# A decoder layer's self attention: the order of the softmax work, of the residual addition and of one unit's transposes

## The chip, the cores and the metric

One core of one Trainium2 chip runs the whole kernel. The metric is the device time of one execution in microseconds; the kernel before is timed three times and its median is taken.

## The reference, cut to what matters

A pre-norm decoder layer on a batch of 32 sequences of 64 tokens, width 512, in float32. It has three parts, each added to the residual x: causal self attention (32 query heads of 16, 8 key heads), cross attention over a context of 64 tokens (32 query heads of 128, 8 key heads, RMS norm of queries and keys), and a feed-forward part with routing. The change is in the first:

```
x = x + attn(layernorm(x), wq, wk, wv, wo)
x = x + cross(layernorm(x), ctx, mask, ...)
x = x + ffn(layernorm(x), ...)

# attn:
scores = einsum('bihd,bjhd->bhij', q, k) * SCALE     # 16 per head, k repeated 4 times
scores = where(causal, scores, finfo.min)
attn   = softmax(scores, axis=-1)
out    = einsum('bhij,bjhd->bihd', attn, v).reshape(b, s, 512) @ wo
```

## The kernel before

The batch is worked in two halves of 16 sequences (1024 tokens, 8 tiles of 128). Each half goes through projections and context transposes, self attention, cross attention (a loop over 8 key heads) and the feed-forward part. Products keep float32 precision by splitting each operand into a high and a low part, so one product is three matmuls (`split_mm`, lines 429 to 431).

Every engine has a list of instructions in program order, written out by hand; an engine waits at a semaphore with all that stands behind it in its list. Self attention is a loop over `p`, one step for each sequence of the half (`NSEQ` = 16), and each engine has its own version of this loop in `self_attention(half)`. A sequence has two units, `2p` and `2p + 1`: the first 32 queries, which see 32 keys (128x256 elements in all), and the last 32, which see all 64 keys (128x512). I call them even and odd units. A unit goes this way:

- TensorE: `scores1(b)`, both units of a sequence, two steps ahead (`AHEAD` = 2), L653 and L657.
- ScalarE: `copy_scores`, L1124, out of the accumulation banks into one of six buffers of `prob`.
- VectorE: `unit_max`, L1562. GpSimd: `unit_subtract_max`, L1930. ScalarE: `unit_exps`, L983. VectorE: `unit_sums`, L1567 and a reciprocal, L1570. GpSimd: `unit_normalise`, L1936.
- TensorE: `transpose_probs`, L470, into one bank (`pt1`) that both units use in turn. ScalarE: `evacuate_probs`, L987. TensorE: `values1`, L675.

After two sequences the output of a token tile is complete: ScalarE's `output_hi` (L990) and VectorE's `output_lo` (L1354) split it, and TensorE projects it in four parts (`project_part`, called from `behind(p, 0)` and `behind(p, 1)`, `y<-w_hi`), two in each of two steps from step 4 on. All these projections use one bank, `y[0]`. VectorE's `updated` (L1574) adds the bank to x and frees it (`y_free`); the first part of the next tile waits for that. From step 7 on VectorE also computes the second layer norm's statistics (`second_statistics`, L1362 to L1367, odd steps) and applies it (`second_norm`, L1584, even steps), with a reciprocal root on GpSimd (L1909) and transposes on TensorE (L689, odd steps from 9). GpSimd's list also splits two weight pieces of the next stage in eight strips (`split_strip`, L1903, steps 5 to 12), and ScalarE casts four pieces (L970, after steps 0, 2, 4 and 7).

In the second half, the projections before self attention are in `second_projections`. There VectorE's list has the low parts of the context tiles (`contexts_lo`, L1354) and two first layer norms (`first_norm(1, 6)` and `first_norm(1, 7)`, L1374). TensorE's transposes of context tiles 4 and 5 (L447) wait for the low parts of tiles 2 and 3, since they use the same two banks.

Of the kernel before, what the change touches and what calls it, by code (L numbers as in the profile page):

```python
# [22 lines left out]
NSEQ = HALF // SEQ  # L23
# [16 lines left out]
AHEAD = 2  # L40
# [80 lines left out]
def decoder_block(nc, x_in, ctx_in, mask_in, w_self, w_cross, qn_in, kn_in, w_ffn,  # L121
                  f1g_in, expt_in, fc2_in, gamma_in, beta_in, out):
    with ExitStack() as stack:
# [164 lines left out]
        def evacuated(eng, at, n):  # L288

            eng.wait_ge(acc_free[n % 2].sem, at(acc_free[n % 2], n // 2 + 1))  # L290
# [136 lines left out]
        def _(pe):  # L427
# [192 lines left out]
            def self_attention(half):  # L620
# [93 lines left out]
                pe.wait_ge(gaps_clear.sem, at(gaps_clear, 1))  # L714

                for p in range(NSEQ + 1):
                    if p + AHEAD < NSEQ:
                        scores1(p + AHEAD)
                    if p >= 1:
                        values1(2 * p - 2)  # L720
                        values1(2 * p - 1)
                    if p == 0:
                        behind(0, 0)
                        evacuated(pe, at, A1[half]["kt1"])
                    if p < NSEQ:
                        transpose_probs(at, 2 * p, (2 * p) % URING)
                    if p > 0:
                        behind(p, 0)
                    else:
                        behind(0, 1)  # L730
                    if p < NSEQ:
                        transpose_probs(at, 2 * p + 1, (2 * p + 1) % URING)
                    if p > 0:
                        behind(p, 1)
                    if p >= 9 and p % 2 == 1:
                        second_norm((p - 9) // 2)
# [228 lines left out]
        def _(act):  # L965
# [19 lines left out]
            def evacuate_probs(at, u, buffer):  # L985
                act.wait_ge(pt_rdy.sem, at(pt_rdy, u + 1))
                nc.scalar.copy(probt[:, buffer, :], pt1).then_inc(pt_done.sem, 1)  # L987
# [116 lines left out]
            def self_attention(half):  # L1104
                place = Place(1, half)
                at = place.at
                def spread_values(b):

                    if b == 0:
                        act.wait_ge(zone_clear.sem, 1)  # L1110
                        act.wait_ge(proj_out.sem, at(proj_out, PROJ[half]["kv3"] + 1))
                    if b >= 4:
                        act.wait_ge(pv_done.sem, at(pv_done, 2 * b - 6))
                    rows = slice((b % 2) * SEQ, (b % 2 + 1) * SEQ)
                    values = kv[rows, b // 2, P:2 * P].rearrange("p (i g d) -> p g i d", i=4, g=2)
                    for g2 in range(2):
                        ins = nc.scalar.copy(own_block(b % 4, g2), values[:, g2])
                    ins.then_inc(vbd_done.sem, 1)

                def copy_scores(u):  # L1120

                    act.wait_ge(sc_rdy.sem, at(sc_rdy, u // 2 * 2 + 2))
                    target = seen(u, u % URING).rearrange("p (i g) k -> p i g k", i=4)
                    nc.scalar.copy(target, far if u % 2 else near).then_inc(s_add.sem, 1)  # L1124

                spread_values(0)
                spread_values(1)
                if half == 0:
                    act.wait_ge(wqk_made.sem, 1)

                    act.wait_ge(f1g_lo_done.sem, 1)
                self_queries(half, 4)
                def second_norm_hi(i):
                    act.wait_ge(solo_rdy.sem, at(solo_rdy, SOLO[f"lx{i}"] + 1))
                    nc.scalar.copy(tile_of(xn_hi, i), blocks(solo)).then_inc(ln_hi_done.sem, 1)

                for p in range(-AHEAD, NSEQ + 1):
                    scored = p + AHEAD < NSEQ
                    if p == -1:
                        self_queries(half, 5)  # L1140
                    if scored:
                        copy_scores(2 * (p + AHEAD))
                        copy_scores(2 * (p + AHEAD) + 1)
                    if 0 <= p < NSEQ:
                        evacuate_probs(at, 2 * p, 0)
                    if scored:
                        unit_exps(at, 2 * (p + AHEAD))
                    if p >= 2 and p % 2 == 0:
                        i = (p - 2) // 2
                        act.wait_ge(pv_done.sem, at(pv_done, 4 * i + 4))  # L1150
                        output_hi(i)
                    if 0 <= p < NSEQ:
                        evacuate_probs(at, 2 * p + 1, 1)
                    if scored:
                        unit_exps(at, 2 * (p + AHEAD) + 1)
                    if p in (1, 3):
                        self_queries(half, 6 + p // 2)
                    if p >= 9 and p % 2 == 1:
                        second_norm_hi((p - 9) // 2)
                    if 0 <= p < NSEQ - 2:  # L1160
                        spread_values(p + 2)
                    if p in (0, 2, 4, 7):

                        n = (0, 2, 4, 7).index(p)
                        if n > 1:
                            act.wait_ge(solo_rdy.sem, at(solo_rdy, 2))
                        else:
                            act.wait_ge(proj_rdy.sem, at(proj_rdy, 8))
                        split_piece(Place(2, half, 0), n)

                first = Place(2, half, 0)
                second_norm_hi(4)
                keys_and_values(first, 0)
                second_norm_hi(5)
                queries(first, 0, 0)
                queries(first, 0, 1)
                second_norm_hi(6)
                keys_and_values(first, 1)
                queries(first, 1, 0)
                sibling_keys(first.at, 0)  # L1180
                queries(first, 1, 1)
                exps(first.at, 0, 0)
                keys_and_values(first, 2)
                sibling_keys(first.at, 1)
                queries(first, 2, 0)
                queries(first, 2, 1)
                second_norm_hi(7)
# [163 lines left out]
        def _(dve):  # L1351
# [107 lines left out]
            def first_norm(half, i):  # L1459
                normalise(Place(1, half).at, 0, i, A1[half][f"ln{i - 2}"] if i >= 2 else None)  # L1460
# [44 lines left out]
            def second_projections():  # L1505
                norms_lo(1, 4)
                contexts_lo(1, 0)
                first_statistics(1, 6)
                first_statistics(1, 7)
                first_norm(1, 6)  # L1510
                first_norm(1, 7)
                contexts_lo(1, 2)
                contexts_lo(1, 4)
                norms_lo(1, 6)
                contexts_lo(1, 6)
# [30 lines left out]
            def self_attention(half):  # L1546
# [44 lines left out]
                first = Place(2, half, 0)  # L1591
                for p in range(-AHEAD, NSEQ + 1):
                    scored = p + AHEAD < NSEQ
                    if scored:
                        unit_max(2 * (p + AHEAD))
                        unit_max(2 * (p + AHEAD) + 1)
                    if p >= 6 and p % 2 == 0:
                        updated((p - 6) // 2)
                    if p >= 11 and p % 2 == 1:
                        second_norm_lo((p - 11) // 2)  # L1600
                    if scored:
                        unit_sums(2 * (p + AHEAD))
                    if p >= 2 and p % 2 == 0:
                        output_lo(at, (p - 2) // 2)
                    if scored:
                        unit_sums(2 * (p + AHEAD) + 1)
                    if p >= 7 and p % 2 == 1:
                        second_statistics((p - 7) // 2)
                    if p >= 8 and p % 2 == 0:
                        second_norm((p - 8) // 2)  # L1610
                    if p in (1, 3):
                        weights_lo(first, p // 2)
# [271 lines left out]
        def _(pool):  # L1884
# [104 lines left out]
            def self_attention(half):  # L1989
# [15 lines left out]
                for p in range(-AHEAD, NSEQ):  # L2005
                    scored = p + AHEAD < NSEQ
                    if scored:
                        unit_subtract_max(at, 2 * (p + AHEAD))
                        unit_subtract_max(at, 2 * (p + AHEAD) + 1)
                    if p >= 8 and p % 2 == 0:  # L2010
                        layernorm_rstd(at, NT, (p - 8) // 2)
                    if scored:
                        unit_normalise(at, 2 * (p + AHEAD))
                        unit_normalise(at, 2 * (p + AHEAD) + 1)
                    if 5 <= p < 13:
                        split_strip(Place(2, half, 0), 2 + (p - 5) // 4, (p - 5) % 4)

# [158 lines left out]
```

## Time and profile before

| | us |
|---|---|
| median of 3 runs | 1632.32 (1631.72 to 1632.89) |
| the profiled execution | 1631.22 |
| its span | 1629.5 |
| TensorE busy in the span | 1572.7 (97%) |
| VectorE, ScalarE, GpSimd busy | 1107.5, 749.3, 618.9 |

The self attention loops lie at 57 to 141 us and 861 to 946 us of the span. Busy time of TensorE is that of pipelined matmuls, whose ends are modelled, so that it hides short pauses. A line in brackets behind a timeline row is the idle time of the engine before that instruction, and what ended it.

### The profile page before, as it was taken

What the parts mean: (1) busy time and instruction counts of PE and PEld (TensorE: products, weight loads), DVE (VectorE), ACT (ScalarE), POOL (GpSimd) and SP (SyncE); (2) the same over time, 40 slices, a digit from 0 to 9 for tenths busy, and PEclk for the clock granted to TensorE, in tenths of its full rate; (3) what the DMA queues carried; (4) which work ended last, traced back from release to release, by engine and by line L of the source; (5) the groups of instructions that cost most, each with busy time, mean ns of one, the idle gap of its engine ahead of it and who ended that gap; (6) DMA issues with size and microseconds to landing.
All of it is one profiled execution on the core that took longest, in us unless ns stands there. A gap on an engine that the chain in (4) does not pass through costs nothing.

```text
span 1629.5 us, 42096 instructions
## 1 busy us (share of the span) xinstructions
PE 1572.7 (97%) x17432; PEld 1317.1 (81%) x17432; DVE 1107.5 (68%) x1965; ACT 749.3 (46%) x1398; POOL 618.9 (38%) x523
## 2 busy tenths in 40 slices
PE   7879999999999999999997799999999999999998
PEld 6557888888888888789885588888888888887897
DVE  6666857667676676785666667667666766768844
ACT  4674535535444444431237645444444544544321
POOL 5573424324243342551227724333243242424501
PEclk9999999999999999999999899999999999999999
DMA  6100202012020120131120002011020110202100
GB/s 226 39 15 7 67 2 65 19 45 64 0 64 19 45 64 6 40 111 52 66 78 27 18 5 67 14 51 57 7 64 6 58 45 19 71 0 66 41 19 27
DMA packets 26289, 71.63 MB, mean 44 GB/s; under 512 B 3168, under 2 KB 3424, under 8 KB 26208
## 3 DMA queue, kind: packets, MB, share of 16 engines
q1 hardware_dynamic: 26208, 70.48, 13.6%
q8 instruction: 60, 0.98, 0.2%
q14 instruction: 21, 0.17, 0.0%
HBM read 66.27 MB, written 4.19 MB: 43 GB/s over the span
## 4 chain that ended last, share of the span: by engine, by line
PE 87%; DVE 4%; POOL 4%; ACT 3%; issue 1%; DMA 0%; SPq 0%; POOLq 0%; ACTq 0%; DVEq 0%
PE acc L429 14%; PE acc L430 13%; PE acc L431 13%; PE y L429 10%; PE y L431 10%; PE y L430 10%; PE quad L781 6%; PE quad L810 4%; PE y L794 2%; POOL prob L1930 2%; POOL prob L1936 1%; ACT prob L983 1%; DVE psum_ L1567 1%; PE acc L447 1%; PE quad L429 1%
## 5 line engine op out<-in xcount | busy, mean ns | idle before, releaser
L429 PE MATMUL y<-w_hi 128*128 128x512 f32 x576 | 231.8, 402 | 23.2 <-DVE x L1574 22.5
L1909 POOL TENSOR_TENSOR qkrs<-qkve,mhalf 128x10 f32<-128x10 f32 x64 | 125.0, 1953 | 302.3 <-DVE qkve L1531 302.3
L431 PE MATMUL y<-w_hi,w_lo 128*128 128x512 f32 x576 | 226.1, 392 | 0.0
L430 PE MATMUL y<-w_lo,w_hi 128*128 128x512 f32 x576 | 225.9, 392 | 0.0
L429 PE MATMUL acc<-w_hi,xn_hi 128*128 128x512 f32 x512 | 207.1, 405 | 0.0
L430 PE MATMUL acc<-w_lo,xn_hi 128*128 128x512 f32 x512 | 201.2, 393 | 0.0
L431 PE MATMUL acc<-w_hi,xn_lo 128*128 128x512 f32 x512 | 199.5, 390 | 0.0
L1430 DVE TENSOR_TENSOR x<-y,x 128x512 f32<-128x512 f32 x128 | 88.3, 690 | 140.3 <-PE y L431 140.3
L1890 POOL TENSOR_TENSOR w_lo<-stage,w_hi 128x1024 fp32r<-128x1024 f32 (+1 forms) x80 | 156.5, 1965 | 62.8 <-ACT w_hi L970 58.8
L1525 DVE TENSOR_REDUCE qkss<-kk 128x4 f32<-128x512 f32 x128 | 87.3, 682 | 103.9 <-ACT kk L1009 103.3
L970 ACT CAST w_hi<-stage 128x1024 fp32r<-128x1024 f32 (+1 forms) x116 | 105.1, 918 | 98.0 <-PE y L431 63.8
L429 PE MATMUL acc<-w_hi,cx_hi 128*128 128x256 f32 x512 | 149.8, 293 | 0.0
L429 PEld LDWEIGHTS y<-w_hi 128*128 128x128 f32 x576 | 109.0, 189 | 48.0 <-issue 23.2
L1918 POOL TENSOR_TENSOR prob<-prob,pmax 128x512 f32<-128x512 f32 x64 | 69.3, 1083 | 201.0 <-DVE pmax L1413 201.0
L431 PE MATMUL acc<-w_hi,cx_lo 128*128 128x256 f32 x512 | 144.9, 283 | 0.0
L430 PE MATMUL acc<-w_lo,cx_hi 128*128 128x256 f32 x512 | 144.8, 283 | 0.0
L1202 ACT COPY probt<-y 128x512 f32<-128x512 f32 x64 | 37.6, 587 | 215.9 <-PE y L794 215.9
L431 PEld LDWEIGHTS y<-w_hi,w_lo 128*128 128x128 f32 x576 | 109.0, 189 | 23.1
L429 PEld LDWEIGHTS acc<-w_hi,xn_hi 128*128 128x128 f32 x512 | 96.0, 187 | 38.7 <-issue 19.2
L430 PEld LDWEIGHTS y<-w_lo,w_hi 128*128 128x128 f32 x576 | 109.2, 190 | 19.9
L1924 POOL TENSOR_TENSOR prob<-prob,prec 128x512 f32<-128x512 f32 x64 | 66.8, 1044 | 153.2 <-DVE prec L1421 153.2
L1008 ACT COPY qb<-acc 128x512 f32<-128x512 f32 x128 | 75.3, 588 | 101.7 <-PE acc L431 98.9
(167 smaller groups left out, 3853.8 us busy)
## 6 DMA issues: line engine op xcount, KB each, us to landing
stage<-in_w_cross SPq DMA_DIRECT2D x64, 512.0 KB, 3.7
stage<-in_w_cross SPq DMA_DIRECT2D x32, 256.0 KB, 2.8
stage<-in_w_ffn SPq DMA_DIRECT2D x16, 512.0 KB, 3.5
stage<-in_w_self SPq DMA_DIRECT2D x8, 512.0 KB, 5.6
out_x<-x SPq DMA_DIRECT2D x16, 256.0 KB, 2.0
x<-in_x SPq DMA_DIRECT2D x6, 512.0 KB, 5.4
kk<-in_ctx SPq DMA_DIRECT2D x8, 256.0 KB, 4.2
prob<-in_ctx SPq DMA_DIRECT2D x8, 256.0 KB, 4.2
```

The source lines that it names most:

```text
L429: nc.tensor.matmul(target, l_hi, r_hi, start=first, stop=False)
L430: nc.tensor.matmul(target, l_hi, r_lo, start=False, stop=False)
L431: return nc.tensor.matmul(target, l_lo, r_hi, start=False, stop=last)
L781: ins = nc.tensor.matmul(quad[h * SEQ:(h + 1) * SEQ, i, t * SEQ:(t + 1) * SEQ], q2t[rows, t, j, 2 * h:2 * h + 2, :].rearrange("p h q -> p ...
L970: nc.scalar.copy(target, stage[:, place.slot(n), 0:width]).then_inc(w_hi_done, 1)
L1008: nc.scalar.copy(qraw[:, 2 * (k % 2) + t], blocks(acc[n % 2]))
L1430: nc.vector.tensor_tensor(x[:, i % NT, :], y[i % 2][:], x[:, i % NT, :], ALU.add).then_inc(y_free.sem, 1)
L1525: nc.vector.tensor_reduce(qkss[:, k % 2, t * REP:(t + 1) * REP], qsq[:, t], AX_X, ALU.add).then_inc(q_sum.sem, 1)
L1890: nc.gpsimd.tensor_tensor(low, stage[:, place.slot(n), 0:width], high.bitcast(F32), ALU.subtract).then_inc(w_lo_done, 1)
L1909: return nc.gpsimd.tensor_tensor(target, source, mhalf[:, 0:width], ALU.pow)
L1918: nc.gpsimd.tensor_tensor(pr, pr, spread(pmax[:, buffer, :], 8, SEQ), ALU.subtract).then_inc(s_sub.sem, 1)
L1924: nc.gpsimd.tensor_tensor(pr, pr, spread(prec[:, buffer, :], 8, SEQ), ALU.mult).then_inc(s_nrm.sem, 1)
```

## The change

Nothing is computed in another way, and no instruction is added or removed. What moves:

- VectorE: `updated` and `second_norm_lo` stand first in the step, ahead of both maxima. The sums of the odd unit are taken one step later.
- TensorE: `scores1(p + 2)` stands behind the even unit's transposes, not at the head of the step. In step 0 two parts of a query projection stand first.
- ScalarE: the even unit's `evacuate_probs` stands ahead of `copy_scores`; the odd unit's exponential moves to the next step, ahead of the even unit's.
- GpSimd: the odd unit's `unit_normalise` moves to the next step, between the two subtractions.
- Second half's projections: `contexts_lo(1, 2)` stands ahead of the two `first_norm`.

```
 TensorE    for p in range(NSEQ + 1):
-                    if p + AHEAD < NSEQ:
-                        scores1(p + AHEAD)
+                    if p == 0:
+                        behind(0, 0)
+                        evacuated(pe, at, A1[half]["kt1"])
+
                     if p >= 1:
                         values1(2 * p - 2)
                         values1(2 * p - 1)
-                    if p == 0:
-                        behind(0, 0)
-                        evacuated(pe, at, A1[half]["kt1"])
                     if p < NSEQ:
                         transpose_probs(at, 2 * p, (2 * p) % URING)
-                    if p > 0:
+                    if p + AHEAD < NSEQ:
+                        scores1(p + AHEAD)
+                    if p == 0:
+                        behind(0, 1)
+                    else:
                         behind(p, 0)
-                    else:
-                        behind(0, 1)
                     if p < NSEQ:
                         transpose_probs(at, 2 * p + 1, (2 * p + 1) % URING)
 ScalarE
+                    if 0 <= p < NSEQ:
+                        evacuate_probs(at, 2 * p, 0)
                     if scored:
                         copy_scores(2 * (p + AHEAD))
                         copy_scores(2 * (p + AHEAD) + 1)
-                    if 0 <= p < NSEQ:
-                        evacuate_probs(at, 2 * p, 0)
-                    if scored:
-                        unit_exps(at, 2 * (p + AHEAD))
+                    if 0 <= p + 1 < NSEQ:
+                        unit_exps(at, 2 * (p + 1) + 1)
...
                     if scored:
-                        unit_exps(at, 2 * (p + AHEAD) + 1)
+                        unit_exps(at, 2 * (p + AHEAD))
 VectorE, second_projections
+                contexts_lo(1, 2)
                 first_norm(1, 6)
                 first_norm(1, 7)
-                contexts_lo(1, 2)
 VectorE, self_attention
-                    if scored:
-                        unit_max(2 * (p + AHEAD))
-                        unit_max(2 * (p + AHEAD) + 1)
+
                     if p >= 6 and p % 2 == 0:
                         updated((p - 6) // 2)
                     if p >= 11 and p % 2 == 1:
                         second_norm_lo((p - 11) // 2)
                     if scored:
-                        unit_sums(2 * (p + AHEAD))
+                        unit_max(2 * (p + AHEAD))
+                    if 0 <= p + 1 < NSEQ:
+                        unit_sums(2 * (p + 1) + 1)
+                    if scored:
+                        unit_max(2 * (p + AHEAD) + 1)
                     if p >= 2 and p % 2 == 0:
                         output_lo(at, (p - 2) // 2)
                     if scored:
-                        unit_sums(2 * (p + AHEAD) + 1)
+                        unit_sums(2 * (p + AHEAD))
 GpSimd
                         unit_subtract_max(at, 2 * (p + AHEAD))
-                        unit_subtract_max(at, 2 * (p + AHEAD) + 1)
                     if p >= 8 and p % 2 == 0:
                         layernorm_rstd(at, NT, (p - 8) // 2)
+                    if 0 <= p + 1 < NSEQ:
+                        unit_normalise(at, 2 * (p + 1) + 1)
                     if scored:
+                        unit_subtract_max(at, 2 * (p + AHEAD) + 1)
                         unit_normalise(at, 2 * (p + AHEAD))
-                        unit_normalise(at, 2 * (p + AHEAD) + 1)
```

## Rows read from the trace of the kernel before

**Rows 1.** Stretch behind the loop: length, busy us PE PEld DVE ACT POOL (instructions), clock
```profile
143.00:164.00 21.00, 21.00 (x123) 18.43 (x123) 12.86 (x29) 9.25 (x19) 3.06 (x3) 1.00 0.00 1
```
**Rows 2.** The same view: both loops, and a slice of the first
```profile
56.60:141.00 84.40, 66.23 (x817) 46.95 (x810) 53.79 (x130) 59.42 (x135) 57.84 (x73) 0.96 0.08 23
860.70:946.50 85.80, 68.02 (x818) 48.33 (x810) 53.78 (x130) 59.58 (x136) 57.87 (x74) 0.92 0.08 23
...
100.00:110.00 10.00, 9.35 (x109) 6.84 (x110) 5.53 (x14) 6.27 (x15) 6.32 (x9) 0.83 0.18 52
```
**Rows 3.** TensorE's waits, first half's loop: total us, times, longest
```profile
PE y L429 <- DVE x L1574: 11.4, 5, 3.4
```
**Rows 4.** Chain that ended last, steps 0 and 1: start, us, what
```profile
60.91 1.58 POOL prob L1930 x2
62.52 0.64 ACT prob L983
63.18 0.70 DVE psum_ L1567
64.18 1.04 POOL prob L1936
```
**Rows 5.** The same chain, steps 9 to 11
```profile
104.86 1.23 POOL prob L1936
...
116.18 1.23 POOL prob L1936
```
**Rows 6.** ScalarE's timeline: start, us, instruction, [idle before, releaser]
```profile
51.14 0.86 ACT L1124 COPY prob<-quad 128x256 f32<-128x256 f32 x2 [0.53 <-PE quad L657]
...
61.84 0.57 ACT L987 COPY probt<-acc 128x512 f32<-128x512 f32 x1
...
95.45 0.57 ACT L987 COPY probt<-acc 128x512 f32<-128x512 f32 x1
...
139.30 0.59 ACT L987 COPY probt<-acc 128x512 f32<-128x512 f32 x1 [0.81 <-PE acc L470]
```
**Rows 7.** TensorE's timeline, first half
```profile
50.26 0.45 PE L653 MATMUL quad<-kk,qb 32*128 32x64 f32 x8
...
62.46 0.43 PE L675 MATMUL acc<-probt,vbd 128*32 128x128 f32 x8 [0.53 <-ACT probt L987]
...
89.24 0.47 PE L429 MATMUL y<-w_hi 128*128 128x512 f32 x1 [1.52 <-DVE x L1574]
...
90.01 0.60 PE L470 MATMUL acc<-ident,prob 128*128 128x128 f32 x4
90.36 0.48 PE L429 MATMUL y<-w_hi 128*128 128x512 f32 x1
...
91.98 0.64 PE L675 MATMUL acc<-probt,vbd 128*32 128x128 f32 x16
92.55 0.66 PE L470 MATMUL acc<-ident,prob 128*128 128x128 f32 x4
```
**Rows 8.** VectorE's timeline, first half
```profile
88.41 0.68 DVE L1574 TENSOR_TENSOR x<-y,x 128x512 f32<-128x512 f32 x1
...
97.64 0.64 DVE L1362 BATCH_NORM_STATS2 bn<-x 128x6 f32<-128x512 f32 x1
...
98.66 1.17 DVE L1562 TENSOR_REDUCE pmax<-prob 128x8 f32<-128x256 f32 x2
```
**Rows 9.** Timelines of TensorE, VectorE, GpSimd, second half's projections
```profile
839.46 1.22 PE L447 MATMUL acc<-ident,kk 128*128 128x128 f32 x8 [1.41 <-DVE cx_lo L1354]
...
835.12 0.55 DVE L1374 TENSOR_SCALAR xn<-x,mv,rstd 128x512 f32<-128x512 f32 x1
836.10 2.60 DVE L1374 TENSOR_SCALAR xn<-x,mv,rstd 128x512 f32<-128x512 f32 x1 [0.44 <-POOL rstd L1909]
...
836.04 2.38 POOL L1890 TENSOR_TENSOR w_lo<-stage,w_hi 128x1024 fp32r<-128x1024 f32 x1
```
**Rows 10.** GpSimd's timeline, first half
```profile
68.49 1.39 POOL L1936 TENSOR_TENSOR prob<-prob,prec 128x512 f32<-128x512 f32 x1 [0.86 <-DVE prec L1570]
```

## The prediction, made before the changed kernel ran

> **What bounds the kernel now.** I read the page first: TensorE is busy for 1572.7 of 1629.5 us, so time can come only from its pauses and from stretches at a low clock. The busy time by stretch shows where these lie: in the two self attention loops TensorE is busy for 66.23 of 84.40 us and for 68.02 of 85.80 us, so it is idle for 18.2 and 17.8 us [rows 2]. In the first loop the list of waits gives the largest part, 11.4 us in five waits of up to 3.4 us, to VectorE's addition to the residual, which frees the one bank of the projections [rows 3]. Such a pause also costs clock: in the slice that holds a pause of 3.4 us the granted clock is 0.83, a part of it at 1.2 instead of 2.4 GHz, and over the whole loops it is 0.96 and 0.92 [rows 2].
>
> The chain of waits shows why VectorE is late. In the first steps it never touches TensorE: GpSimd subtracts the maxima of two units (1.58), ScalarE takes the odd unit's exponential (0.64), VectorE sums it (0.70 and 0.30 to GpSimd's start), GpSimd normalises it (1.04), and only then comes the next subtraction: 1.6 + 0.7 + 1.0 + 1.0 = 4.3 us for one step, in series [rows 4]. Late in the loop two steps take 116.18 - 104.86 = 11.3 us [rows 5], 5.7 each. TensorE is not needed for a step longer than about 4 us: values 0.57, transposes 0.35 to 0.4 twice, scores 0.8 (a little less than the 0.88 from their start to their copy at 51.14, [rows 6]), two parts of a projection at 0.77 each [rows 7] make 3.7.
>
> I take as the clock of the loop ScalarE's copy of the odd unit's transposes (the odd copy). Before, it starts at 61.84 in step 0, at 95.45 in step 7 and at 139.30 in step 15 [rows 6]: 33.6 us for seven steps and 43.9 for eight.
>
> **The odd unit's end one step later.** GpSimd's list is now: subtract even, normalise the last odd, subtract odd, normalise even. The odd unit's exponential and sum run beside two GpSimd instructions of the next step. What is left in series for an odd unit is subtraction 1.0, exponential 0.66, sum 1.0, normalisation 1.0, 3.7 us [rows 4], 0.6 less than before, and it starts a step earlier than it is needed. GpSimd's own work, 57.8 us in 16 steps [rows 2], is 3.6 a step and no longer sets the pace, but leaves little slack.
>
> Next late are ScalarE and TensorE in turn. After an odd copy: 0.62 to the values (61.84 to 62.46, [rows 6, 7]), 0.57 for them, 0.4 for the even transposes, 0.88 from the scores' start to their copy (50.26 to 51.14, [rows 6, 7]), then on ScalarE two score copies and the odd exponential (0.86 and 0.64, of which about 0.2 overlap: 1.3), then the next odd copy. That is 3.8 us; in an even step the output's high part, a copy like the odd copy (0.6, less 0.1 of overlap), stands in between: 4.3. Seven steps: 3 x 4.3 + 4 x 3.8 = 28.1; with ScalarE's weight casts behind steps 0, 2 and 4, mostly beside TensorE's values, I take 28.3. Gain 5.3 us.
>
> **Step 0.** Two query parts stand first and fill the pause in which the scores wait for a copy. The first odd copy now waits for GpSimd: normalise unit 1, subtract unit 3, then ScalarE's exponential. I put it at 60.0 instead of 61.84. Gain 1.9. The even unit 2 is normalised later than before and still ahead of its transposes; with that cover gone each microsecond there would count once.
>
> **The addition first.** The change takes two maxima (1.17, [rows 8]), and what they wait for, from in front of it. Still in front of it stands the end of VectorE's odd step: the even unit's sum and the statistics (97.64 to 98.66, 1.0, [rows 8]). So the wait for it does not vanish from step 8 on. From the odd copy: 0.75 until the even exponential starts (behind the odd copy on ScalarE), 0.45 for it and 0.6 for the sum with its reciprocal (estimates, from 0.64 and 0.70 for the odd unit's twice as many elements, [rows 4]), 0.2 behind the odd maximum, 1.0 for the statistics, 0.83 from the addition's start to TensorE (88.41 to 89.24, [rows 7, 8]), 0.77 for the part, 0.66 for the transposes until the next odd copy [rows 7]: 5.3 us for an even step. TensorE alone would need some 1.2 us less, so I expect four waits of 1.1 to 1.7 us, none in step 6, which has no statistics in front. An odd step is TensorE's own, 3.7 and 0.1 of hops, 3.8; the last, without scores, 3.0. Steps 8 to 15: 5.5 (a weight cast in front) + 5.4 + 5.3 + 4.8 (no scores) + 3 x 3.8 + 3.0 = 35.4. Gain 43.9 - 35.4 = 8.5. The pauses get too short for the low clock: the 1.52 us one in front of 89.24 left the next matmul at 0.47 [rows 7].
>
> The even transposes in front of the scores cost nothing as long as their unit is normalised, and it is, two steps ahead. The scores start some 0.4 us later after them; this is in the 0.4 above. No DMA is issued by any step that moves. The weight strips on GpSimd and the second norm's transposes are in the steps as before; behind the loop TensorE is busy for all of 21 us [rows 1], so nothing waits there that VectorE could bring earlier.
>
> **One half, the other half.** 1.9 + 5.3 + 8.5 = 15.7 us for the first loop. The second is 1.4 us longer, at the lower clock [rows 2]; without the low clock it loses that too: 17.1. In the second half's projections TensorE waits 1.41 us for the low parts of the context [rows 9]; with these in front of the two norms the wait goes, 1.4. The norms move back by some 0.6 us beside the same long GpSimd instruction (836.04, 2.38 us), which sets the second's end rather than the order [rows 9]. Sum 34.2.
>
> From this I take 4 for what the rows show once and the sum has not: GpSimd's normalisation takes 1.39 us instead of 1.04 beside some VectorE instructions [rows 4, 10], which I put at 0.25 in eight steps of each loop. An estimate, bounded by 0 and by 0.35 x 32 steps = 11.
>
> The bounds of the whole: all idle time of both loops, 36.0, the 1.4, and up to 5 of clock (the loops' lower clock took 1.8 more busy time in the second than in the first [rows 2]) would be 42.4; below, the early gain alone, 2 x 7.2 less 1 of clock, 13. Forecast 34.2 - 4 = 30. The profiled execution took 1631.22, so 1601.2; its median stands 1.1 above, so **1602.3 us**.
>
> **Rivals.** *TensorE fills up*: hops overlap better and the waits for the addition go wholly. For it: no engine but TensorE needs over 4 us a step. Against: statistics stand in front of the addition. Gain 41, 1591 us.
>
> *The addition stays late*: the wait of even steps keeps its length because the even unit's sum, which now waits for an exponential behind two copies, comes as late as both maxima did. For it: the serial 5.3 us is an addition of hops, each of which may be short. Then the late gain is gone: 13 to 14, 1618 us.
>
> *No change that can be told*: the loop is paced by something that isn't moved. Only ScalarE's work, 59.4 us in 84.4 [rows 2], comes near, and it leaves 25. 1632.
>
> *Slower: VectorE and GpSimd get into each other's way.* Before, GpSimd stands idle when VectorE writes the second norm (L1584); after, it is busy some 85% of the loop (57.8 of about 69). A write of the same size and kind took 0.55 us beside an idle GpSimd, and 2.60 when a GpSimd instruction of 2.38 us had begun 0.06 before it [rows 9]. If each of the 16 in the two loops is drawn out by 2.05, on the path, that is 33 us and eats the whole gain: 1632.3 - 30 + 33 = 1635. It decides at a mean of about 2.4 us for L1584. Against: GpSimd's instructions in the loop last 1.04 at most, and these writes stand in even steps' ends, in front of a maximum with slack.
>
> The Trainium skill, GPSIMD Engine Reference, section "Key points", says that GpSimd shares its SBUF interfaces with VectorE and is in contention with VectorE instructions that run in a 2-port mode or have two SBUF inputs. The trace agrees in the 2.60 against 0.55; by that rule as a full lock the slower rival would hold, and by the rows' length of GpSimd's instructions in the loop, 1.04 at most, it costs half of that or less.
>
> **Chances.** Forecast 0.62, fills up 0.15, addition stays late 0.13, no change 0.03, slower 0.07. Range 1590 to 1620: it takes in the fuller and the late rival and leaves out no change and slower, and a tenth in sum. What this kernel's measurement can tell from no change is about 0.2%, 3.3 us. Faster by more: 0.90; within: 0.03; slower by more: 0.07.
>
> **What would show it.** Odd copies of the first half at about 60, 88 and 124 us, against 61.84, 95.45 and 139.30; the loop's end near 125. Waits of TensorE for L1574: four of 1.1 to 1.7 in each half, about 5.5 in all. Granted clock 1.00 in both loops. No wait of L447 for the low context parts in the second half. GpSimd without its 0.86 us wait in front of each odd normalisation [rows 10]. Wrong: if even steps take 6 us or more, if L1584 is over 1.5 us in the mean, or if time is given back behind the loop, where TensorE has no pause now [rows 1].

## The result and the profile after

The changed kernel takes 1616.59 us in the median of five runs (1615.12 to 1625.62), against 1632.32: ratio 0.992, 95% interval 0.9906 to 0.9934. By the interval it is faster by 11 to 15 us, by the medians by 15.7; forecast were 30, to 1602.3. The median lies in the range of 1590 to 1620, but about half of the forecast gain is missing. A second set of six runs of the same kernel had a median of 1621.64 (1613.32 to 1628.65).

The profiled execution is the slowest of the first five, 1625.62 us. TensorE's waits in both loops, from the list of waits of the kernel after (what waits and for what: us in total, times, longest); the lines of the page and of the code are one to three higher than before, so L1575 is the addition, L1355 the subtraction behind `output_lo`, L675 the values:

```profile
PE acc L675 <- DVE w_lo L1355: 16.9, 12, 2.2
PE y L429 <- DVE x L1575: 8.6, 8, 1.6
PE acc L675 <- ACT probt L988: 2.9, 4, 1.1
```

The waits for the addition have shrunk from 22.5 us in both loops (11.4 in the first, [rows 3]) to 8.6, a little below the forecast of some 5.5 in each. A wait that was 1.0 us in all before is now the largest: TensorE's values (the products of probabilities and values, `values1`) wait for VectorE's low part of the output, 16.9 us in twelve waits. In step 3 of the first half it looks like this, in ScalarE's timeline:

```profile
66.99 0.63 ACT L984 ACTIVATE prob<-prob 128x512 f32<-128x512 f32 x1 [0.26 <-POOL prob L1933]
67.53 0.57 ACT L991 CAST w_hi<-acc 128x512 fp32r<-128x512 f32 x1
```

in VectorE's:

```profile
67.65 0.69 DVE L1568 TENSOR_REDUCE psum_<-prob 128x8 f32<-128x512 f32 x1 [0.96 <-ACT prob L984]
...
68.49 0.63 DVE L1563 TENSOR_REDUCE pmax<-prob 128x8 f32<-128x512 f32 x1
69.04 0.68 DVE L1355 TENSOR_TENSOR w_lo<-acc,w_hi 128x512 fp32r<-128x512 f32 x1
```

and in TensorE's:

```profile
69.87 0.96 PE L675 MATMUL acc<-probt,vbd 128*32 128x128 f32 x16 [2.15 <-DVE w_lo L1355]
70.76 1.12 PE L470 MATMUL acc<-ident,prob 128*128 128x128 f32 x4
```

The values of a new tile go into the bank that holds the output of the last one, and may not start until both of its parts are out. The high part now stands behind the odd unit's exponential on ScalarE; the low part stands behind that unit's sum and the next odd maximum on VectorE, so that it starts 0.94 us after the high part's end (68.10 to 69.04). In the kernel before, at the same place, ScalarE, VectorE and TensorE had:

```profile
70.81 0.57 ACT L990 CAST w_hi<-acc 128x512 fp32r<-128x512 f32 x1
```

```profile
71.51 0.64 DVE L1354 TENSOR_TENSOR w_lo<-acc,w_hi 128x512 fp32r<-128x512 f32 x1
```

```profile
72.30 0.65 PE L675 MATMUL acc<-probt,vbd 128*32 128x128 f32 x16 [0.24 <-DVE w_lo L1354]
```

There the low part also had two maxima and a sum in front of it, but both maxima were done at 70.07 and the sum was the even unit's, so the low part started 0.13 us behind the high one. Behind the pause of 2.15 us the values take 0.96 and the transposes 1.12 us instead of 0.64 and 0.66 [rows 7]. The busy time by stretch shows a low granted clock there (bounds, length, busy us of PE, PEld, DVE, ACT, POOL, granted clock, DMA):

```profile
70.00:80.00 10.00, 10.00 (x106) 7.21 (x101) 4.16 (x10) 5.63 (x13) 5.16 (x7) 0.66 0.06 12
80.00:90.00 10.00, 8.20 (x76) 5.52 (x75) 5.61 (x13) 6.46 (x15) 5.90 (x8) 0.69 0.11 44
```

The odd copies of steps 0, 7 and 15, which were the clock of the prediction [rows 6], in ScalarE's timeline:

```profile
59.57 0.57 ACT L988 COPY probt<-acc 128x512 f32<-128x512 f32 x1
...
98.78 0.59 ACT L988 COPY probt<-acc 128x512 f32<-128x512 f32 x1
...
137.54 0.59 ACT L988 COPY probt<-acc 128x512 f32<-128x512 f32 x1 [0.81 <-PE acc L470]
```

59.6, 98.8 and 137.5 where 60, 88 and 124 were expected. Steps 0 to 2 are within half a microsecond of the working (63.32 and 67.99 follow); from step 3 on the measured steps are longer.

### The profile page after: what moved, and what is told of

Same layout as the page of the kernel before. It is cut to its first block, busy times and chain, and to the rows that moved or that the text cites. A ratio compares the mean times of both kernels' runs of the same rounds, so it can differ in the third digit from the quotient of the medians.

```text
span 1623.9 us, 42096 instructions
## 1 busy us (share of the span) xinstructions
PE 1578.9 (97%) x17432; PEld 1322.4 (81%) x17432; DVE 1106.5 (68%) x1965; ACT 748.8 (46%) x1398; POOL 619.0 (38%) x523
## 4 chain that ended last, share of the span: by engine, by line
PE 92%; DVE 3%; ACT 3%; issue 1%; POOL 1%; DMA 0%; SPq 0%; POOLq 0%; ACTq 0%; DVEq 0%
PE acc L429 14%; PE acc L430 13%; PE acc L431 13%; PE y L429 10%; PE y L430 10%; PE y L431 10%; PE quad L782 6%; PE quad L811 4%; PE y L795 2%; PE acc L470 1%; PE quad L653 1%; PE acc L447 1%; PE quad L429 1%; PE acc L675 1%; PE quad L431 1%; PE quad L430 1%
```

## Experiments

All times are medians, set against runs of the kernel before on the same chip: 1631.89 us for the first four, 1631.23 for the last four.

**The changed kernel once more.** No edit.

> The changed kernel as it is. Its five times lay from 1615.1 to 1625.6 us, and the profiled execution was the slowest, with granted clock 0.66 to 0.69 in two slices of the first loop. Theory A: the spread is the low clock, which some executions catch behind the 2 us waits for output_lo in steps 3 and 5; then another execution of about 1615 us shows the same waits of TensorE (L1355 some 16 us in both loops, L1575 some 9) and a granted clock near 1.00 in the loops, which are then some 4 to 5 us shorter each. Theory B: the waits themselves differ between executions, and the clock is only a mark of it.

Measured: 1621.64 us (1613.32 to 1628.65, six runs), ratio 0.9942 (0.9919 to 0.9965). Time and the mean granted clock of the execution go together: 1613.32 and 1614.76 at 0.999, 1621.25 and 1622.02 at 0.993, 1626.6 at 0.990, 1628.65 at 0.988. The profiled execution was the fastest. Its waits, and its two loops by busy time:

```profile
PE acc L675 <- DVE w_lo L1355: 15.8, 12, 2.1
PE y L429 <- DVE x L1575: 10.0, 10, 1.6
```

```profile
54.00:142.00 88.00, 73.58 (x881) 54.29 (x882) 60.51 (x150) 62.88 (x143) 59.90 (x76) 0.98 0.08 23
857.00:947.00 90.00, 76.68 (x880) 58.47 (x877) 61.18 (x148) 60.87 (x138) 57.36 (x72) 1.00 0.07 22
```

The same stretches in the profile of 1625.62 us:

```profile
54.00:142.00 88.00, 73.66 (x865) 53.08 (x858) 57.39 (x138) 61.51 (x140) 59.22 (x75) 0.92 0.07 22
857.00:947.00 90.00, 75.86 (x861) 55.42 (x861) 58.74 (x144) 60.04 (x137) 58.86 (x74) 0.91 0.07 22
```

The same twelve waits of up to 2.2 us in both profiled executions, with a loop clock of 0.98 and 1.00 in one and of 0.92 and 0.91 in the other. Theory A holds for these two: the waits are there both times, the clock falls behind those of steps 3 and 5 in one and not in the other. The times of one and the same kernel spread over 15 us. The fastest execution is 18.6 us below the median of the kernel before (whose mean clock is 0.991 to 0.994), the slowest 3.2.

**The output's split earlier.**

```
 ScalarE
+   output_hi(i)                                # with its wait
     if 0 <= p + 1 < NSEQ: unit_exps(at, 2 * (p + 1) + 1)
-   output_hi(i)
 VectorE
     if scored: unit_max(2 * (p + AHEAD))
+   output_lo(at, (p - 2) // 2)
     if 0 <= p + 1 < NSEQ: unit_sums(2 * (p + 1) + 1)
     if scored: unit_max(2 * (p + AHEAD) + 1)
-   output_lo(at, (p - 2) // 2)
```

> The changed kernel with the output's split earlier: ScalarE's output_hi ahead of the odd unit's exponential, VectorE's output_lo ahead of the odd unit's sum and maximum. Theory A (the missing gain lies in TensorE's wait for output_lo, 16.9 us in twelve waits, and in the low clock that the long ones bring): that wait falls below 3 us, odd steps take 3.8 to 4.0 us instead of 4.9, and the time is 1600 to 1606 us. Theory B (the odd steps are bound by the softmax chain itself, and the wait for output_lo only stands in front): the wait moves to the odd unit's copy or its transposes, and the time stays at 1612 to 1616.

Measured: 1600.87 us (1599.00 to 1601.06), ratio 0.9804 (0.9791 to 0.9816), clock 0.997 to 0.999 in every run. The list of waits, then TensorE's timeline at the values of step 3, then ScalarE's odd copies:

```profile
PE y L429 <- DVE x L1575: 10.8, 10, 1.6
PE acc L675 <- ACT probt L988: 2.9, 4, 1.1
PE acc L675 <- DVE w_lo L1355: 1.2, 4, 0.3
```

```profile
67.55 0.74 PE L675 MATMUL acc<-probt,vbd 128*32 128x128 f32 x16 [0.33 <-DVE w_lo L1355]
```

```profile
59.03 0.57 ACT L988 COPY probt<-acc 128x512 f32<-128x512 f32 x1
...
87.72 0.59 ACT L988 COPY probt<-acc 128x512 f32<-128x512 f32 x1
...
125.61 0.59 ACT L988 COPY probt<-acc 128x512 f32<-128x512 f32 x1 [0.81 <-PE acc L470]
```

The wait falls from some 16 us to 1.2, and the time to that of the forecast: 31 us gained. Theory A holds. Against the two executions of the changed kernel at a mean clock of 0.999 (1613.32 and 1614.76) it is 12 to 14 us, near the 14.6 us of waiting that are gone (15.8 to 1.2); what the medians show beyond that goes with the clock. The odd copies at 59.0, 87.7 and 125.6 lie close to the 60, 88 and 124 of the prediction. Step 11 takes 3.9 us from odd copy to odd copy (103.90 to 107.84), where the changed kernel has 4.9 (113.92 to 118.82). What ScalarE's part of this edit brings alone was not measured.

The low clock has become rarer and is not gone. TensorE's timeline and the stretch around it:

```profile
91.77 0.47 PE L429 MATMUL y<-w_hi 128*128 128x512 f32 x1 [1.48 <-DVE x L1575]
```

```profile
90.00:100.00 10.00, 8.52 (x94) 6.16 (x92) 6.58 (x18) 7.53 (x17) 7.79 (x11) 0.83 0.08 17
```

**Only the low part, ahead of the odd maximum.** In VectorE's list `output_lo` changes places with `unit_max(2 * (p + AHEAD) + 1)`; ScalarE as in the change.

> The changed kernel with VectorE's output_lo ahead of the odd unit's maximum only (0.55 us earlier); ScalarE unchanged. Theory A: each of the twelve waits for output_lo shrinks by 0.55, 6.6 us in all, more where that also keeps the clock up: 1606 to 1610 us. Theory B (the maximum, now 0.6 us later, holds up GpSimd's subtraction and so the step): no gain, 1615 or more.

Measured: 1605.87 us (1605.41 to 1607.81), ratio 0.9841 (0.9828 to 0.9854), clock 0.998 to 1.000. That is 8 us below the changed kernel at its high clock, close to the 6.6 of twelve half microseconds, and 11 to 16 below its medians, which have the low clock in them. Waits:

```profile
PE y L429 <- DVE x L1575: 10.0, 10, 1.6
PE acc L675 <- ACT vbd L1118: 5.9, 4, 1.6
PE acc L675 <- DVE w_lo L1355: 3.0, 6, 0.9
```

The values wait for 5.9 + 3.0 us here, 6.9 less than the 15.8 at high clock. The profile puts four of these waits to copies of values into `vbd`, which belong to a later sequence. In step 3 the low part ends at 68.57 and the values start at 68.72, the same 0.15 us after it as in the changed kernel (69.72 and 69.87), so I read them as waits for it. One maximum, 0.63 us long, has moved by one place: theory A, and a dose between nothing and the experiment before.

**The addition first, alone.** The kernel before, with `updated` and `second_norm_lo` ahead of both maxima.

> The kernel before with one part of the change alone: VectorE's addition to the residual (and second_norm_lo) ahead of both maxima. Theory A: it takes the two maxima, 1.0 us, and what they wait for from ten waits of 22.5 us, and leaves the sum and the statistics in front; the softmax ring of 5 us a step stays: 8 to 12 us gained, 1620 to 1624 us, some from the clock. Theory B (the ring of the softmax sets late steps too, the wait for the addition moves to the odd unit's transposes): under 4 us, 1628 to 1632.

Measured: 1626.37 us (1624.84 to 1627.43), ratio 0.9964 (0.9952 to 0.9977). Waits:

```profile
PE y L429 <- DVE x L1574: 16.4, 10, 2.3
PE acc L470 <- ACT probt L987: 5.0, 7, 1.0
```

Between the theories: 5.5 us gained, from 6.1 us less of waiting for the addition. The waits shrink by 0.6 us each rather than by the 1.0 of the two maxima; the even unit's sum and the statistics stand in front as before. The waits for the low part grow from 1.0 to 2.5 us.

**The second half's context edit, alone.** The kernel before, with `contexts_lo(1, 2)` ahead of the two norms.

> The kernel before with the edit of the second half's projections alone (low parts of context tiles 2 and 3 ahead of two layer norms). Theory A: TensorE's wait of 1.4 us there goes and nothing else moves: 1630.0 to 1631.0 us against 1631.9, at the edge of what can be told; in the profile L447 waits for L1354 no more. Theory B: the time is given back at the next transposes, 1631.9.

Measured: 1632.03 us (1627.60 to 1634.10, eleven runs), ratio 0.9998 (0.9988 to 1.0007). The wait of 1.41 us [rows 9] is in no list of waits of this kernel or of the changed one, but the time can't be told from before; the interval allows a gain of up to 2.0 us, so 1.4 is neither shown nor excluded in the whole time. The granted clock of its runs is 0.989 to 0.993, and their times spread over 6.5 us. In the profiles the gain can be seen: from the transposes in front of the ones that waited to the first even copy of the second half's loop it is 29.35 us before (834.26 to 863.61) and 27.54 here (837.06 to 864.60), so up to the loop nothing of it is given back.

**The statistics behind the addition.** The kernel with the output's split early, and VectorE's `second_statistics` moved:

```
     if p >= 6 and p % 2 == 0: updated((p - 6) // 2)
     if p >= 11 and p % 2 == 1: second_norm_lo((p - 11) // 2)
+   if p >= 8 and p % 2 == 0: second_statistics((p - 8) // 2)
...
-   if p >= 7 and p % 2 == 1: second_statistics((p - 7) // 2)
```

> The kernel with the output's split early (1600.9 us), and the second norm's statistics moved from the end of VectorE's odd step to behind the addition in the even step. Theory A (what holds the addition up is the statistics in front of it, 1.0 us): the ten waits of TensorE for L1575, 10.8 us, fall below 3 us, and the time to 1592 to 1596 us. Theory B (VectorE's even step is then too full, 5.2 us of work against a step of 4.3): the wait moves to the low part or to the odd unit's transposes, 1598 to 1602.

Measured: 1597.03 us (1596.33 to 1597.64), ratio 0.9787 (0.9774 to 0.9801), the fastest of all; it beats the kernel before by 34 us and the changed one by 20. Waits:

```profile
PE y L429 <- DVE x L1575: 5.4, 10, 1.0
PE acc L675 <- DVE w_lo L1355: 3.6, 10, 0.7
```

Between the theories: half of the waits for the addition goes, and 2.4 of the 5.4 us come back as waits for the low part, as B said. The gain is 3.8 us, of which the lists account for 3.0; the profiled execution is the only one with a granted clock of 1.00 in both loops, against 0.98 in the kernel it started from. That VectorE's list is now too full, as B has it, fits this but is not shown.

**The addition put back behind the maxima, in the changed kernel.** `updated` (the addition) and `second_norm_lo` stand behind `unit_max(2 * (p + AHEAD) + 1)`, so behind the odd sum too.

> The changed kernel with the addition (and second_norm_lo) put back behind both maxima; the odd unit's end still one step later. It shows what the part named first in the change is worth inside it. Theory A (two reasons add): the waits for the addition grow by 1.9 us each (two maxima and an odd sum now stand in front) in ten steps, and the clock falls in most executions: 1633 to 1645 us, so that the deferral without it gains nothing. Theory B (the deferral alone carries the gain): 1616 to 1622.

Measured: 1663.32 us (1661.40 to 1663.98), ratio 1.0191 (1.0177 to 1.0205), clock 0.979 to 0.981. Worse than both theories had it. Waits up to 950 us of the span, then an even step's addition in VectorE's timeline and the projection behind it in TensorE's:

```profile
PE y L429 <- DVE x L1575: 30.0, 8, 4.0
PE acc L675 <- DVE w_lo L1355: 8.1, 4, 2.2
PE y L689 <- DVE xn_lo L1355: 5.1, 3, 1.7
```

```profile
108.79 0.68 DVE L1575 TENSOR_TENSOR x<-y,x 128x512 f32<-128x512 f32 x1
```

```profile
109.62 0.77 PE L429 MATMUL y<-w_hi 128*128 128x512 f32 x1 [3.95 <-DVE x L1575]
```

With the odd unit's end one step later (the deferral) but the addition not first, the kernel is 32 us slower than before; with the addition first it is faster. The eight waits listed are 3.75 us in the mean, and all runs have a low clock. I had 1.9 us more a wait; it is over 2.5. In front of the addition now stand a maximum that waits for the score copies and a sum that waits for the odd exponential of the same step; I take that as the reason, no run separates them. A wait for `second_norm_lo`, 5.1 us in three, is new.

**TensorE's scores back at the head of the step.** The kernel with the output's split early, and in steps 1 to 13 `scores1(p + AHEAD)` ahead of the values.

> The kernel with the output's split early (1600.9 us), and TensorE's scores of step p + 2 put back to the head of the step, ahead of values and even transposes (step 0 stays as changed). It shows what TensorE's part of the order is worth. Theory A (the scores fill the time in which TensorE waits for the odd copy, so their place is worth little or even a gain): 1598 to 1603 us. Theory B (the even transposes, 0.75 us later, hold up the even and then the odd copy in every step): 0.4 to 0.75 us in 28 steps, 1612 to 1622.

Measured: 1606.37 us (1606.10 to 1608.51), ratio 0.9848 (0.9835 to 0.9862), 5.5 us more than with the scores behind the even transposes (7 by the ratios). Waits:

```profile
PE y L429 <- DVE x L1576: 13.9, 10, 2.0
PE acc L470 <- ACT probt L989: 3.0, 8, 0.6
```

Neither theory: the place costs 0.2 us a step, not 0.4 to 0.75, and it is not free. TensorE fills with the scores the time in which it would wait for the odd copy, as A said (L675 waits 0.8 instead of 2.9 us for L989), but it waits 0.3 us longer for each addition (13.9 against 10.8 us) and 3.0 us, which were not there, for copies in front of its transposes. In all, the waits in the two lists grow by 2.8 us of the 5.5 (14.9 to 17.7, with the 1.2 for the low part gone); the rest stays open.

## Why the prediction was wrong

- The place was right: the self attention loops. In the fastest execution (1613.32 us) the odd copy of step 15 starts at 132.65 in the first half, 6.7 us earlier than before, and at 927.22 in the second, 17.5 earlier than before (944.74), and behind it next to nothing more is gained (17.9 in all); 15.7 and 34.2 less 4 were forecast.
- **The step that failed** is the one that begins "Next late are ScalarE and TensorE in turn". It let the values follow the odd copy by 0.62 us. In odd steps from 3 on they wait for the low part too. The change puts the odd sum, which waits for the odd exponential, in place of the even sum in front of it, and the odd maximum behind that sum instead of ahead; in the kernel before the low part followed the high part by 0.13 us and cost 1.0 us of waiting in all. I worked out what the addition has in front of it, and not what `output_lo`, which is not in the diff as a moved line but has other lines around it, has in front of it. Twelve waits of 16 to 17 us in all, with the low clock behind the long ones, are the missing half: taken away, the time is 1600.9 us against 1602.3 forecast. Two doses show it: a part of the wait taken away gives 1605.87, nearly all of it 1600.87.
- A second step failed with it, "The pauses get too short for the low clock", and the granted clock of 1.00 in both loops. Behind the new waits of 2.1 us in steps 3 and 5 there are 0.66 and 0.69 in two slices of one execution, which is 12 us longer than the one without. And the clock fell behind a shorter wait too: in the kernel with the output's split early the slice with the wait of 1.48 us has 0.83, and each loop 0.98.
- That 1600.9 lies so near 1602.3 is in part luck. From odd copy to odd copy, steps 10 to 13 of that kernel's first half take 5.28, 3.94, 5.29 and 3.93 us, as worked out (5.4, 3.8, 5.3, 3.8), but steps 8 and 9, where the clock fell, take 10.9 instead of 9.3, and step 14 takes 5.3 instead of 4.8. The 4 us taken off at the end cover this. They were meant for GpSimd's normalisation at 1.39 instead of 1.04 us, and that did not come: none took over 1.07 us in the changed kernel, and none over 1.25 in this one.
- The odd unit's end one step later: the first steps are as worked out, with odd copies at 59.57, 63.32 and 67.99. GpSimd's wait of 0.86 us before each odd normalisation [rows 10] was to go; it is 0.55 in the first steps, about 0.9 in most later ones and gone in three of the even steps.
- Step 0: 1.9 us forecast, 2.3 measured (61.84 to 59.57), of which 0.3 were there before the loop began.
- The addition first: four waits of 1.1 to 1.7 us in each half, 5.5 a half, were forecast; 8 to 10 of up to 1.6, 8.6 to 10.0 us in both halves together, were measured: near the forecast, which is 11 for both. Alone it is worth 5.5 us; put back inside the change it costs 42 to 47. The two parts of the change do not simply add up: the deferral lengthens what stands in front of an addition that is not first (3.75 us a wait), and only with the addition first was it a gain.
- TensorE's order: costed at nothing, with its reasons. In the kernel with the output's split early it is worth 5.5 to 7 us.
- The context edit: its wait is gone, and the stretch up to the loop is 1.8 us shorter in the profile of this edit alone; in the whole time its 1.4 us can't be told.
- The rivals. "The addition stays late" named a time near the measured one, 1618, by the wrong instruction; its waits did shrink. "Slower: VectorE and GpSimd get into each other's way" did not come: L1585 took 0.54 to 0.98 us, 0.66 in the median, against 0.50 to 0.54 before, far from the 2.4 from which it would decide. Two of its readings were wrong: before, GpSimd did not stand idle through all these writes (a normalisation starts at 104.86, 0.16 us after VectorE's write began), and its instructions in the loop are not 1.04 us at most, since [rows 5] and [rows 10] have 1.23 and 1.39. "TensorE fills up" was out of reach; the statistics later came nearest, at 1597.0.

## What to carry to other kernels

When instructions in an engine's list change places, go through every instruction of the list that has new neighbours in front of it, not only through those that move. Ask of each who waits for it, and what its new neighbours wait for: here as many instructions stood in front of the low part as before, and it still came later. Before you defer work in an engine's list, look for a release (a bank, a buffer) that ends up behind it: here the medians were 10 to 16 us below the kernel before with the addition first, and 32 above it with the addition (and the second norm's low part) behind the maxima. And where times of one kernel spread by 15 us, compare the granted clock of the executions first.

## What the runs showed of the hardware

A pause of TensorE of about 2 us does not always lower its clock: the same waits of 2.1 us were followed by 0.66 in one execution and by nearly full clock in another, and one kernel's times spread over 1613 to 1629 us with mean clocks of 0.999 to 0.988. Shorter pauses do not exclude it: slices with granted clock 0.83 hold waits of 1.48 us (the output's split early) and 1.63 us (only the low part). In the three kernels whose waits in the loops were 1.6 us at most, it came more rarely: the mean clock stayed at 0.997 or above and the times of one kernel within 2.4 us. Only the one with the statistics later, with waits of 1.1 us at most, had 1.00 in both loops.

VectorE's `TENSOR_SCALAR` of 128x512 (L1585) takes 0.54 us beside an idle GpSimd. Beside a busy one it takes up to 0.98 us in the changed kernel, and up to 1.38 in the one with the statistics later. VectorE's and GpSimd's timelines, first of the changed kernel, then of that one:

```profile
105.63 0.97 DVE L1585 TENSOR_SCALAR xn<-x,mv,rstd 128x512 f32<-128x512 f32 x1
...
105.28 1.05 POOL L1933 TENSOR_TENSOR prob<-prob,pmax 128x512 f32<-128x512 f32 x1
```

```profile
105.44 1.38 DVE L1585 TENSOR_SCALAR xn<-x,mv,rstd 128x512 f32<-128x512 f32 x1
...
105.50 1.05 POOL L1933 TENSOR_TENSOR prob<-prob,pmax 128x512 f32<-128x512 f32 x1
```

In both it ends some 0.27 us after a GpSimd instruction ends (106.60 and 106.33; 106.82 and 106.55), and so do the other stretched writes of L1585 in these two traces, by 0.27 to 0.29 us; so does the write of 2.60 us [rows 9] (838.70 and 838.42). In the kernel before, where it started 0.16 us ahead of GpSimd, VectorE's instruction was not stretched and GpSimd's was, to 1.23 us [rows 5] from 1.04:

```profile
104.70 0.50 DVE L1584 TENSOR_SCALAR xn<-x,mv,rstd 128x512 f32<-128x512 f32 x1
```

In the second pair GpSimd was still at the instruction before (104.49 to 105.53) when VectorE's began. So in these rows it is the instruction that begins while the other engine is at work that gets longer. No experiment took GpSimd's work away, so that this is the cause is read from the profiles, not shown by a run.
